# A fused attention and expert kernel: gathers paced by late units, and half of the held weight splits moved from the projection stage to the early units

## What is computed

```python
x = x + xattn(layernorm(x), ctx, ctx, Wq, Wk, Wv, Wfc, bfc)     # 32 heads in 8 groups, 16 dims each
h = layernorm(x)
scores = softmax(h @ gate_weight.T)                             # 8 experts in 4 groups
topk_w, topk_i = group_limited_topk(scores)                     # best 2 groups, best 2 experts
wmat = (one_hot(topk_i) * topk_w[..., None]).sum(1)
e = einsum('ntf,nhf->nth', silu(h @ gate_w.T) * (h @ up_w.T), down_w)
routed = einsum('nth,tn->th', e, wmat)
shared = silu(h @ sh_gate.T) * (h @ sh_up.T) @ sh_down.T        # width 704, done as two experts of 352
x = x + routed + shared
```

## Time and profile before

| | |
|---|---|
| time, 3 runs | 776.47, 780.15, 780.23 us (median 780.15) |
| profiled execution | 776.41 us, of which the span of the core 774.3 us |
| mean granted clock of TensorE | 0.985 |
| busy, share of the span | PE 95%, PEld (weight loads) 52%, DVE 73%, ACT 54%, POOL 35% |
| chain that ended last, by engine | PE 63%, DVE 19%, DMA 9%, issue 5% |

### The profile page before, as it was taken

The page is one execution under the profiler, slowest core; times in us unless marked ns, Lnnn a source line. Parts: engine busy times, 40 slices in busy tenths (PEclk is TensorE's granted clock), DMA queues, the critical chain, the costliest instruction groups (busy, mean ns, idle before and its releaser), DMA issues.

```text
span 774.3 us, 16113 instructions
## 1 busy us (share of the span) xinstructions
PE 737.8 (95%) x5325; PEld 399.1 (52%) x5326; DVE 562.1 (73%) x1191; ACT 418.6 (54%) x845; POOL 271.2 (35%) x221
## 2 busy tenths in 40 slices
PE   5998989999999999999999999999999999993998
PEld 4553533434444345656665665555555666550455
DVE  5677799999999878787699986555555555451676
ACT  3666578888888856775634554343434333210222
POOL 3263007999995303656003111111111110167000
PEclk9999999999999999999999999999999999996799
DMA  9998857576555889995785656777777795497663
GB/s 331 348 404 246 257 158 212 157 205 186 173 162 160 291 321 370 367 368 201 188 251 170 176 135 163 173 184 172 183 174 182 172 214 129 128 282 244 184 173 92
DMA packets 155099, 168.15 MB, mean 217 GB/s; under 512 B 97952, under 2 KB 111776, under 8 KB 154528
## 3 DMA queue, kind: packets, MB, share of 16 engines
q1 hardware_dynamic: 143724, 126.20, 55.6%
q0 software_dynamic: 10720, 40.12, 16.6%
q10 hardware_dynamic: 596, 1.07, 0.4%
HBM read 104.09 MB, written 41.42 MB: 188 GB/s over the span
## 4 chain that ended last, share of the span: by engine, by line
PE 63%; DVE 19%; DMA 9%; issue 5%; SPq 2%; ACT 2%; DVEq 0%; ACTq 0%
PE psum L1522 28%; PE psum L1539 15%; DVE sb_rows L1787 11%; PE psum L1524 4%; PE psum L1258 4%; PE psum L1449 3%; DMA sb_weights<-k_parts 3%; PE psum L1541 2%; DMA sb_weights<-in_wdn 2%; DMA sb_rows<-xb_dram 2%; PE psum L1234 2%; DMA sb_weights<-in_x 1%; DVE sb_rows L1916 1%; PE psum L1282 1%; PE psum L1239 1%
## 5 line engine op out<-in xcount | busy, mean ns | idle before, releaser
L1522 PE MATMUL psum<-sb_weights,sb_rows 128*128 128x352 f16 (+1 forms) x1344 | 214.6, 315 | 7.7 <-issue 7.6
L1522 PEld LDWEIGHTS psum<-sb_weights,sb_rows 128*128 128x128 f16 x1344 | 131.7, 98 | 87.1 <-issue 12.1
L1787 DVE TENSOR_REDUCE sb_rows<-psum 128x4 f32<-128x1024 f32 x128 | 149.8, 1213 | 5.1 <-PE psum L1282 5.1
L1074 ACT ACTIVATE sb_weights<-psum 128x512 f32<-128x512 f32 x256 | 139.5, 595 | 22.4 <-PE psum L1354 19.5
L1539 PE MATMUL psum<-sb_weights,sb_hT 128*128 128x512 f16 (+1 forms) x522 | 125.0, 383 | 7.2 <-issue 7.0
L1148 ACT ACTIVATE psum<-psum 128x352 f32<-128x352 f32 x68 | 30.5, 448 | 129.0 <-DVE psum L2041 122.9
L933 POOL DMA_INDIRECT sb_rows<-xn_rows,sb_slot_tok x36 | 34.7, 963 | 176.6 <-DVE sb_rows L2419 134.8
L1354 PE MATMUL psum<-sb_weights 50*128 50x512 f16 x256 | 86.0, 384 | 1.7 <-ACT sb_weights L1074 0.9
L1539 PEld LDWEIGHTS psum<-sb_weights,sb_hT 128*128 128x128 f16 x522 | 50.9, 98 | 65.3 <-issue 12.7
L1368 PE MATMUL psum<-sb_weights 128*32 128x256 f32 x1024 | 81.8, 391 | 0.3
L1282 PE MATMUL psum<-sb_weights 48*128 48x256 f16 x512 | 70.0, 272 | 1.9 <-DMA sb_weights<-k_parts 1.1
(11 more groups left out here) (307 smaller groups left out, 1172.0 us busy)
## 6 DMA issues: line engine op xcount, KB each, us to landing
sb_weights<-in_wgu SPq DMA_DIRECT2D x20, 704.0 KB, 8.6
sb_weights<-in_wgu POOLq DMA_DIRECT2D x20, 704.0 KB, 6.9
sb_weights<-in_wdn SPq DMA_DIRECT2D x17, 768.0 KB, 6.0
slot_y<-sb_rows SPq DMA_DIRECT2D x36, 256.0 KB, 2.4
sb_weights<-q_parts SPq DMA_DIRECT2D x96, 64.0 KB, 3.2
x_dram<-sb_rows SPq DMA_DIRECT2D x24, 256.0 KB, 4.5
q_parts<-sb_weights SPq DMA_DIRECT2D x16, 256.0 KB, 5.9
sb_rows<-in_x POOLq DMA_DIRECT2D x16, 256.0 KB, 5.5
```

The source lines that it names most:

```text
L1074: nc.scalar.activation(probs[G % 2][:, kt, pair * 512:(pair + 1) * 512], bank[4 + f % 2], ACT.Exp, scale=exp_by[n]).then_inc(exp_done, 1)
L1522: mm = nc.tensor.matmul(to[:, 0:F], x_T[:, at:at + P], gu(wp, k, which), start=first, stop=last)
L1787: nc.vector.tensor_reduce(to[:, :, j // UB, :, j % UB, qt], psum[:, banks[qt] * 512:(banks[qt] + 2) * 512] .rearrange("p (a h k) -> p a h ...
```

## The change

Two parts.

*Gathers.* Every pair of gathers q waits until C0 + 3 + (2q div 3) units have finished their gate_up; before, only q = 1, 2 and 3 had such a wait.

*Held halves.* Only five of the ten (the first half of each of the five experts) are loaded and split in the projection stage, all five on ScalarE and GpSimd; VectorE's `second_part` is gone. The other five are loaded by GpSimd's queue into the places of down weights 5, 6 and 7 (two once all projections are done, one once 4 units' gate_ups are done, two more when a place is free again); ScalarE makes their high parts in units 2 to 6 between silu and square, GpSimd their low parts in two instructions each. To leave these places free, SyncE loads routed down weights 0 to 3 in units 1 to 4 and 4 to 6 in units 9 to 11, behind a wait for the last split. `cut_down` begins in unit 7 and leaves out 8 and 10. The iotas for the routing stand behind the second of the five splits on GpSimd's queue.

```diff
@@ -77,8 +77,9 @@
 FREE = 16
 HELD = 5
 CUTS_P2 = CUTS - 2 * HELD
+HELD_PLACES = (5, 7, 6, 5, 7)
 EARLY = TILES // 2
-CUT_W = 8
+CUT_W = 7
 PA, PB, PC = SH * EARLY, SLOTS, SH * (TILES - EARLY)
 
...
+        cut_order = list(range(2 * HELD, CUTS)) + list(range(0, 2 * HELD, 2)) + list(range(1, 2 * HELD, 2))
+
+        def held_stage(k):
+
+            return stage_p3[k % 3] if k < HELD else words(DN0 + HELD_PLACES[k - HELD] * DN_W, HALF)
...
                 if e < NE - 1:
-                    sp.dma_start(dn_raw(e + 1), wdn[e]).then_inc(dn_ld_late if e in (5, 6) else dn_ld, 16)
+                    sp.dma_start(dn_raw(e + 1), wdn[e]).then_inc(dn_ld_late if e >= 4 else dn_ld, 16)
...
                 if w == 2:
-                    sp.wait_ge(gu_cut, CUTS - HELD)
-                    sp.wait_ge(gu_cut_v, HELD)
+                    sp.wait_ge(gu_cut, CUTS_P2 + HELD)
                     sp.wait_ge(fc_ready, TILES)
                     sp.wait_ge(xb_done, TILES)
-                if w == 6:
-                    sp.wait_ge(u_ready, 4)
-                if 1 <= w < 8:
+                if w == 9:
+                    sp.wait_ge(gu_cut, CUTS)
+                if 1 <= w < 5:
                     load_down(w - 1)
+                if 9 <= w < 12:
+                    load_down(w - 5)
...
-            def load_held(h):
-                nc.gpsimd.dma_start(stage_p3[h % 3], wgu[h // 2, :, h % 2 * HALF:(h % 2 + 1) * HALF]).then_inc(gu_ld[h % 3], 16)
+            def load_held(k):
+                h = cut_order[CUTS_P2 + k]
+                nc.gpsimd.dma_start(held_stage(k), wgu[h // 2, :, h % 2 * HALF:(h % 2 + 1) * HALF]).then_inc(gu_ld[k % 3], 16)
...
-                pool.wait_ge(gu_scaled, pool_cuts(c))
+                pool.wait_ge(gu_scaled, c + 1)
                 nc.gpsimd.tensor_tensor(low, stage, high, ALU.subtract).then_inc(gu_cut, 1)
-                pool.wait_ge(gu_cut, pool_cuts(c))
+                pool.wait_ge(gu_cut, c + 1)
...
-            for h in range(3):
-                load_held(h)
-            for c in range(CUTS_P2, CUTS):
-
-                h = c - CUTS_P2
-                if h % 2 == 0:
-                    scale_weights(c)
-                    second_part(c)
-                else:
-                    pool.wait_ge(gu_cut_v, h // 2 + 1)
-                if h + 3 < 2 * HELD:
-                    load_held(h + 3)
+            for k in range(3):
+                load_held(k)
+            for k in range(HELD):
+                scale_weights(CUTS_P2 + k)
+                second_part(CUTS_P2 + k)
+                if k + 3 < HELD:
+                    load_held(k + 3)
             for c in range(SH):
                 dn_second(NE + c, c + 1, [dn_raw((NE + c) % 3)])
 
-            pool.wait_ge(pre_ready, 1)
-            nc.gpsimd.iota(lane_iota, [[1, P]], base=0, channel_multiplier=0,
-                           allow_small_or_imprecise_dtypes=True).then_inc(iotas, 1)
-            nc.gpsimd.iota(tok_id, [[P, TILES]], base=0, channel_multiplier=1,
-                           allow_small_or_imprecise_dtypes=True).then_inc(iotas, 1)
+            pool.wait_ge(fc_ready, TILES)
+            for k in range(HELD, HELD + 2):
+                load_held(k)
+            pool.wait_ge(u_ready, 4)
+            load_held(HELD + 2)
+            for k in range(HELD, 2 * HELD):
+                scale_weights(CUTS_P2 + k)
+                second_part(CUTS_P2 + k)
+                if k < HELD + 2:
+                    load_held(k + 3)
+                if k == HELD + 1:
+                    pool.wait_ge(pre_ready, 1)
+                    nc.gpsimd.iota(lane_iota, [[1, P]], base=0, channel_multiplier=0,
+                                   allow_small_or_imprecise_dtypes=True).then_inc(iotas, 1)
+                    nc.gpsimd.iota(tok_id, [[P, TILES]], base=0, channel_multiplier=1,
+                                   allow_small_or_imprecise_dtypes=True).then_inc(iotas, 1)
             dn_second(0, SH + 1, [dn_raw(1)])
...
             for q in range(2 * EARLY):
                 t = q // 2 + q % 2 * EARLY
+                pool.wait_ge(u_ready, C0 + 3 + 2 * q // 3)
                 if q >= 4:
                     pool.wait_ge(gat_ld[q % 4], q // 4 * 32)
-                elif q > 0:
-                    pool.wait_ge(u_ready, C0 + 2 + q)
...
-            def first_part(h):
-
-                act.wait_ge(gu_ld[h % 3], (16 * CUTS_P2 // 2 if h % 3 < 2 else 0) + h // 3 * 16 + 16)
-                nc.scalar.activation(cut_place(h)[0], stage_p3[h % 3], ACT.Copy,
+            def first_part(k):
+
+                h = cut_order[CUTS_P2 + k]
+                act.wait_ge(gu_ld[k % 3], (16 * CUTS_P2 // 2 if k % 3 < 2 else 0) + k // 3 * 16 + 16)
+                nc.scalar.activation(cut_place(h)[0], held_stage(k), ACT.Copy,
                                      scale=w_scale[:, h // 2:h // 2 + 1]).then_inc(gu_first, 1)
...
-                if t - 2 < 2 * HELD:
-                    first_part(t - 2)
+                if t % 2 == 0 and t - 2 < 2 * HELD:
+                    first_part((t - 2) // 2)
...
-                    act.wait_ge(dn_ld, 16 * (NE - 3))
+                    act.wait_ge(dn_ld, 16 * (NE - 4))
                 else:
                     act.wait_ge(dn_cut, SH + e)
-                if e == 5:
-                    act.wait_ge(dn_ld_late, 32)
+                if e == 4:
+                    act.wait_ge(dn_ld_late, 48)
...
             for w in range(2, B0):
-                e = w - CUT_W if w < CUT_W + 2 else w - CUT_W - 1
-                unit(w, w % 2, w // 2, shared_inv(w % 2), None if w < CUT_W or w == CUT_W + 2 else lambda: cut_down(e))
+                k = HELD + w - 2
+                e = {CUT_W: 0, CUT_W + 2: 1}.get(w, w - CUT_W - 2)
+                between = None
+                if k < 2 * HELD:
+                    between = lambda: first_part(k)
+                elif w not in (CUT_W + 1, CUT_W + 3):
+                    between = lambda: cut_down(e)
+                unit(w, w % 2, w // 2, shared_inv(w % 2), between)
...
             pe.wait_ge(offs_done, 1)
-            pe.wait_ge(gu_cut, CUTS - HELD)
-            pe.wait_ge(gu_cut_v, HELD)
+            pe.wait_ge(gu_cut, CUTS)
             slot_up(0, 0)
...
-            def second_part(h):
-
-                dve.wait_ge(gu_first, CUTS_P2 + h + 1)
-                high, low = cut_place(h)
-                nc.vector.scalar_tensor_tensor(low, stage_p3[h % 3], w_scale[:, h // 2:h // 2 + 1], high,
-                                               ALU.mult, ALU.subtract).then_inc(gu_cut_v, 1)
-
             for t in range(2, TILES):
                 residual_norm(t, t % 2, t // 2)
-                if t % 2 == 1 and t < 2 * HELD + 2:
-                    second_part(t - 2)
```

7 lines of the change are left out of this document (2 added, 5 removed).

## The result

Twenty runs of each kernel were timed in turn. The changed kernel takes 781.51 us (777.33 to 787.97), the kernel before 778.01 us (775.11 to 781.34): ratio 1.0041, 95% interval 1.0022 to 1.0059, slower by 3.5 us. Its profiled execution took 783.61 us, with a span of 781.5 us, 7.2 us over the span of the kernel before; it is a run from the upper part of its twenty, so of these 7.2 us about half are the choice of the execution.

What follows compares the result with a forecast made beforehand. TensorE, busy for 95% of the span, was taken as the bound. From the profiled 776.4 us: -22.85 (stall), +1 (gather users), -1.3 (projection), +25 (VectorE's port waits), +1 (clock) gave 779.2 us, range 755 to 800.

Steps and rivals of the forecast that it cites:

- its own case: Whole kernel: both large terms, stall gain and port loss, come out near their size; 773 to 785 us, chance 0.46.
- The reference: Whole kernel: sum made from the profiled execution's 776.4 us, then compared with the median 780.15 and the lowest run 776.47.
- Stall gone, -22.85: Late units: pacing stops the gathers' burst from accumulating, so TensorE's idle gaps go; -22.85 us, bounds 0 and 22.85 gained.
- The rival of a slow first pass of the loop: Late units: instruction fetch in the loop's first pass causes the stall, so pacing leaves it; 801 us, no separate chance.
- VectorE waits for the port, +25: Early units: VectorE instructions with two SBUF inputs, short ones too, wait for GpSimd's splits; +25 us, bounds 0 and 27.
- the term for the lower clock (+1): Early units: TensorE falls to its lower clock after standing 5 to 8 us at a time; +1 us, bounds 0 and 4.
- the walk: Early units: queues of four engines followed unit by unit with timeline durations; 26.3 us more on VectorE, or 22.
- Projection stage, -1.3: Projection stage: TensorE already sets the pace, so removing five halves gains little; -1.3 us, bounds 0 and -2.
- Users of the paced gathers, +1 (0 to 4): Late units: VectorE waits for later gathered rows in early_out, late_out and late_gathered; +1 us, bounds 0 and 4.
- The parts costed at nothing: Early units: loads, ScalarE's first parts, SyncE's new wait and late down loads stay hidden; 0 us, bound +3.
- Short instructions don't wait: Early units: the stall goes and short VectorE instructions do not wait for GpSimd; 753.3 us, chance 0.14.
- the stall stays, in part or whole: Late units: gathers still fill the DMA engines; half the stall kept 790 us, chance 0.15; whole 801 us, chance 0.15.

Runs made afterwards that it cites:

- pace_again: Kernel before with only the gathers' pacing added, run where the kernel before stalls: 766.12 and 752.98 us.
- held_again: Changed kernel with the gathers' pacing taken back to the unpaced burst, run where the kernel before stalls: 806.78 us, ratio 1.034 to the kernel before.
- burst_late: Kernel before with one more wait, gathers from the fifth pair on held until a later late unit, stall present: 775.09 us, ratio 0.994.
- before_again: Kernel before, unchanged, run and traced again on an occasion with the stall: 777.05 us.
- held_only: Changed kernel with the gathers' pacing taken back to the unpaced burst, run where the kernel before does not stall: 784.14 us, ratio 1.037 to it.
- after_again: Changed kernel, unchanged, run and traced again on an occasion where the kernel before stalls: 780.47 us.
- after_third: Changed kernel, unchanged, run once more where the kernel before does not stall: 779.89 us, ratio 1.028 to the kernel before.
- copy_splits: Changed kernel with GpSimd's arithmetic for the five early halves replaced by DMA copies (output not the reference's): 762.65 us.
- vector_splits: Changed kernel with the five early second parts done by VectorE, one instruction each, instead of GpSimd: 766.79 us, ratio 1.013 to a kernel before without stall.

## Why the prediction was right and wrong, point by point

The predicted time, 779.2 us, lies 2.3 us under the measured 781.5, inside the range and inside the narrower range of its own case. The direction was missed: "faster 0.36, same 0.22, slower 0.42" leaned the right way, but the time itself was set just under the 780.15 us of the three runs shown, and the kernel is slower. Both mechanisms were right. The step that failed is the last one, the reference; the terms of the sum were off by up to 2.5 us beside it.

- **The reference: the step that failed.** The sum was made against an execution of 776.4 us, the lower end of the runs, then set beside a median of three at 780.15 and read as -0.1%. The sum itself says +2.85 us against its own execution. Measured are +3.5 us between the medians of twenty (778.01 and 781.51) and +7.2 between the two traces. Setting +2.85 against a higher median turned a small loss into a small gain. The same paragraph gives +0.4% against the lowest run, and that one was the right reading.
- **Stall gone, -22.85.** Right in cause where the kernel before stalls, by pace_again, held_again and burst_late; right in size for this execution (25.2 us in before_again). What the profile of before could not show is that the stall is only there on some occasions. Where it is absent the term is about nothing and the change costs 22 us. The reason given, that the burst has to add up and the busy DMA is not what matters, fits held_only, where the DMA share was higher (1.07) and nothing stalled; but the same run shows that the burst alone doesn't suffice. The rival of a slow first pass of the loop is refuted by burst_late.
- **VectorE waits for the port, +25.** Right: 24.9 us more of waiting on VectorE. With the term for the lower clock (+1) the sum has 26, and the early stage was 26.7 us longer, 26.9 in after_again and 27.5 in after_third; so the clock and what comes with it were put 1 to 1.5 us too low. The step on which the term hung, that short instructions wait as long as long ones, is shown by L2116 and L2117 above. The Trainium skill, in "SBUF — State Buffer", the section "Who interferes with whom", speaks of such an exclusive lock, and the trace agrees: 2.55 and 2.88 us for 0.29. In one point the walk had it otherwise: it let only instructions with two SBUF inputs wait, and four of the ten waits are those of copies with one. Each of these copies stands just ahead of an instruction with two, so by the walk's rule the sum would be much the same. TensorE's gaps were 2.4 to 5.8 us, not 5 to 8.
- **Projection stage, -1.3.** Right, 1.3.
- **Users of the paced gathers, +1 (0 to 4).** Wrong waiter, and no steady size: 3.45 us in the profiled execution, 0.1 us or less in after_again and after_third. VectorE waiting for its rows was costed; what TensorE waits for, where it waits, is hT transposes. The DMA share doesn't decide it: from 700 to 750 us it was 1.02 with the wait, and 0.99 and 1.04 in the two traces without one. Why the transposes come late in some executions stays open.
- **The parts costed at nothing.** ScalarE's first parts, the loads and SP's wait cost nothing that the changed kernel's profile shows; with the port out of the way about 2 us of DMA wait appear (copy_splits, vector_splits), within the bound of 3. The slots' stage was put at nothing by silence and is 0.6 us longer in all three traces of the changed kernel (230.2 or 230.3 us for 229.6), unexplained.
- **The rivals.** "Short instructions don't wait" (753 us) and "the stall stays, in part or whole" (790, 801) are both refuted for this kernel. The whole stall beside the early loss is what held_again has, with the burst put back: 806.8 us.

## What to carry to other kernels

Two parts of one change can each be worth 3% and cancel: here the pacing alone, 753.7 us (10 runs; 753.0 and 766.1 where the kernel before takes 780), is the better kernel on both kinds of occasion, some 27 us ahead of the changed kernel by the ten runs, and about even with the kernel before (0.9965, 0.993 to 1.0) where that doesn't stall. Before work goes to GpSimd beside a VectorE without slack, count each GpSimd instruction on SBUF at its full duration on VectorE's path, short VectorE instructions and copies with one SBUF input included; moving the same work to the full VectorE cost less than half (12.6 us for 26.7). A duration read beside another engine's work can hold a wait: the split on VectorE takes 1.67 us, and 2.0 to 2.8 where GpSimd splits too. Take the reference for a small forecast from the execution that the sum was made against, as a difference.

## What was new about the hardware

- **Gathers can hold back TensorE's instructions, on some occasions only.** With 32 gathers of 128 rows, one each 1.25 us, idle gaps of 0.2 to 2.4 us with no releaser set in 12 to 15 us behind the start of its unbroken part and last until 4 to 5.5 us past the start of its last gather. The gaps add up to 14.6 us in the kernel before and 17.8 in before_again, and with the lower clock behind them they cost 22.85 and 25.2 us. Four of seven occasions had it (kernel before at 777 to 780 us), three not (757 us), with one chip on both lists. The same burst without a stall is in held_only's trace, at a higher DMA share (1.07 for 0.90). What differs between occasions was not found, and no run was made for it.
- Plain loads of the same bytes did not do it (one run on an occasion with the stall), but took 9 to 15 us more than a kernel before without the stall, because the hT transposes came late, by up to 7.1 us each.
- Four gathers a unit of 5.52 us gave four gaps of 1.75 us together, three gave none.
- A copy on VectorE with one SBUF input (128 x 8 to 128 x 64 float32, 0.17 to 0.20 us alone) that meets a GpSimd tensor_tensor takes until that one ends, 2.06 to 2.74 us, as an instruction with two SBUF inputs does; a reduce of an SBUF tensor (0.27 us) and instructions with one PSUM input (0.59, 0.74 us) pass it.
